# Mamba stage of a decoder kernel: silu taken by ScalarE's own function, the residual added by TensorE, the x product and GpSimd's share of the read-outs moved

## The reference, cut to what matters

```python
residual = hidden + residual
hidden = _layernorm(residual, norm_w[i], norm_b[i])
xin, z = jnp.split(jnp.einsum('bld,ed->ble', hidden, in_w), 2, axis=-1)   # 2 x 256 channels
xc = silu(causal_conv(xin, cw, cb))                                       # 4 taps
dtr, Bm, Cm = split(jnp.einsum('bld,ed->ble', xc, xp_w))                  # 8, 16, 16
dt = softplus(jnp.einsum('blr,dr->bld', dtr, dtp_w) + dtp_b)
h = exp(dt * A) * h + (dt * xc) * B        # a scan over time, for 16 states
y = sum over the 16 states of h * C, + xc * D
hidden = jnp.einsum('bld,ed->ble', y * silu(z), out_w)
```

## Time and profile before

| | |
|---|---|
| time, three runs | 8373.63 / 8380.08 / 8388.14 us |
| time of the profiled execution | 8408.26 us |
| its span, first to last instruction | 8406.3 us |
| mean granted clock of PE | 0.856 of full speed |
| busy in the whole span | PE 76%, DVE 80%, ACT 52%, POOL 58% |
| Mamba rounds | from 112.0 to 4187 us, 64 rounds |

### The profile page before, as it was taken

How to read it: one execution, slowest core, us unless ns; L and a number is a source line. 1 busy time by engine, 2 the same in 40 slices (tenths; PEclk the granted TensorE clock), 3 DMA queues, 4 the chain that set the end, 5 groups by cost and what they waited for, 6 DMA issues and landing times. The chain is left out here.

```text
span 8406.3 us, 94285 instructions
## 1 busy us (share of the span) xinstructions
PE 6429.7 (76%) x25844; PEld 3390.0 (40%) x25859; DVE 6708.0 (80%) x15635; ACT 4403.6 (52%) x9194; POOL 4877.1 (58%) x2829
## 2 busy tenths in 40 slices
PE   5888888888888888888789967777656777777745
PEld 2333333333333333333355545555433444455522
DVE  5999999999999999999855558888666767767657
ACT  3555555555555555555555523333325666666633
POOL 4888878888788888888744434444212333333310
PEclk9998899889888889988889978888757989989955
DMA  5333333333433333333310047777310000000011
GB/s 183 136 149 157 138 145 143 152 143 145 156 135 149 153 141 139 146 157 135 143 32 26 20 122 204 206 205 204 109 44 17 10 9 9 9 9 9 6 32 36
DMA packets 373729, 896.56 MB, mean 107 GB/s; under 512 B 28031, under 2 KB 270076, under 8 KB 306972
## 3 DMA queue, kind: packets, MB, share of 16 engines
q1 hardware_dynamic: 332508, 692.64, 22.0%
q0 software_dynamic: 40960, 201.36, 8.3%
HBM read 850.58 MB, written 56.77 MB: 108 GB/s over the span
## 5 line engine op out<-in xcount | busy, mean ns | idle before, releaser
L380 POOL TENSOR_TENSOR mb_dBu<-mb_dtu,mb_rows_b 128x1024 f32<-128x1024 f32 x1027 | 2406.5, 2361 | 360.9 <-DVE mb_bank L394 186.5
L394 DVE TENSOR_TENSOR_SCAN mb_bank<-mb_bank,mb_dBu 128x1024 f32<-128x1024 f32 x704 | 1612.7, 2291 | 71.8 <-PEq L63 50.9
L434 PE MATMUL mb_bank<-mb_hcd,ident 128*128 128x512 f32 x2560 | 1269.6, 623 | 76.7 <-DVE mb_hcd L408 76.7
L365 ACT ACTIVATE mb_bank<-mb_dt,mb_a_neg 128x508 f32<-128x508 f32 x2050 | 1312.4, 671 | 0.8
L434 PE MATMUL mb_bank<-mb_hcp,ident 128*128 128x512 f32 x1280 | 792.5, 752 | 366.2 <-POOL mb_hcp L417 366.2
L417 POOL TENSOR_TENSOR mb_hcp<-mb_hs,mb_rows_c 128x1024 f32<-128x1024 f32 x320 | 753.0, 2353 | 354.9 <-DVE mb_hs L394 351.7
L408 DVE TENSOR_TENSOR mb_hcd<-mb_bank,mb_rows_c 128x1024 f32<-128x1024 f32 x704 | 862.1, 1225 | 31.3
L434 PEld LDWEIGHTS mb_bank<-mb_hcd,ident 128*128 128x128 f32 x2560 | 501.3, 202 | 793.3 <-issue 588.4
L1542 POOL DMA_INDIRECT ex_rows<-in_ex_table,ex_idx x512 | 490.1, 957 | 560.3 <-DVE ex_idx L1538 345.2
L394 DVE TENSOR_TENSOR_SCAN mb_hs<-mb_bank,mb_dBu 128x1024 f32<-128x1024 f32 x320 | 730.9, 2284 | 40.1 <-ACT mb_bank L365 40.1
L434 PEld LDWEIGHTS mb_bank<-mb_hcp,ident 128*128 128x128 f32 x1280 | 282.0, 234 | 815.2 <-POOL mb_hcp L417 494.7
(11 more groups left out here) (369 smaller groups left out, 13434.8 us busy)
## 6 DMA issues: line engine op xcount, KB each, us to landing
mb_rows_b<-bc_rows SPq DMA_DIRECT2D x259, 1024.0 KB, 7.4
mb_rows_c<-bc_rows SPq DMA_DIRECT2D x258, 1024.0 KB, 6.8
stream<-mb_r_post SPq DMA_DIRECT2D x69, 256.0 KB, 2.4
mb_r_tok<-stream SPq DMA_DIRECT2D x67, 256.0 KB, 2.8
mb_r_post<-stream SPq DMA_DIRECT2D x65, 256.0 KB, 2.8
ex_rows<-in_ex_table,ex_idx POOLq DMA_INDIRECT x512
tj_x_tok<-stream SPq DMA_DIRECT2D x17, 256.0 KB, 3.1
bc_rows<-mb_xp SPq DMA_DIRECT2D x65, 64.0 KB, 1.6
```

The lines of the kernel that those rows point to most:

```text
L365: e = nc.scalar.activation(da_of(n)[:, c * GB:(c + 1) * GB, 1:], dt[q][:, c].rearrange("p (b t) -> p b t", b=GB)[:, :, 1:], ACT.Exp, scale ...
L380: nc.gpsimd.tensor_tensor(by_c(dBu[m % RING][:]), by_c(chains(dtu[q][:])), over_c(rows_b[:, n]), ALU.mult).then_inc(s["mb_dbu"], 1)
L394: nc.vector.tensor_tensor_scan(flat(to), flat(da_of(n)), flat(dBu[n % RING][:]), 0.0, ALU.mult, ALU.add).then_inc(s["mb_scan"], 1)
L434: m = nc.tensor.matmul(bank[:, B_Y + c], ident[:], part[:, c * GB:(c + 1) * GB], start=False, stop=False)
```

## The change

In the Mamba stage alone:

- Silu of the convolution is one ACT instruction per half with function Silu, straight into `u`; both stand after step 3's `act_da`. `dve_conv` is gone. Silu of z is one ACT instruction over both halves; `dve_z` is gone. The weights lose their factors.
- The residual is added by PE: a product of the identity with the old rows (`r_old`, a buffer of its own) opens the accumulation in bank `M1`, ahead of `pe_out`. ACT copies the sum out (`act_new`, after its step 1) in place of DVE's addition.
- PE's convolution of the second half stands right after `pe_out`, ahead of the skip products, and the x product after the sum of step 2 (it was after step 4's place).
- POOL reads out the states 1, 5, 8, 10 and 12 (they were 2, 4, 8, 10 and 12).

```diff
-ON_POOL = (2, 4, 8, 10, 12)
+ON_POOL = (1, 5, 8, 10, 12)
...
             def act_conv(self, act, c):
                 act.wait_ge(s["mb_conv"], c + 1)
-                nc.scalar.activation(th[:, c], bank[:, M0 + c], ACT.Tanh, scale=0.5, bias=conv_bh[:, c:c + 1]).then_inc(s["mb_tanh"], 1)
-                act.wait_ge(s["mb_tanh"], c + 1)
-                nc.scalar.activation(th[:, c], th[:, c], ACT.Identity, bias=1.0).then_inc(s["mb_th"], 1)
...
+                nc.scalar.activation(u[self.q][:, c], bank[:, M0 + c], ACT.Silu, bias=conv_b[:, c:c + 1]).then_inc(s["mb_u"], 1)
...
             def act_z(self, act):
...
+                act.wait_ge(s["mb_z"], CH)
+                nc.scalar.activation(zg[self.q][:], x_psum, ACT.Silu).then_inc(s["mb_zg"], 1)
...
             def pe_out(self, pe):
+                pe.wait_ge(s["mb_rp"], 16)
+                nc.tensor.matmul(bank[:, M1], ident[:], r_old[:].rearrange("p b d -> p (b d)"), start=True, stop=False)
                 pe.wait_ge(s["mb_yg"], 1)
...
-            def dve_add(self, dve):
-                dve.wait_ge(s["mb_out"], 1)
-                dve.wait_ge(s["mb_rp"], 16)
...
+            def act_new(self, act):
+                act.wait_ge(s["mb_out"], 1)
+                nc.scalar.activation(r_post[:].rearrange("p b d -> p (b d)"), bank[:, M1], ACT.Copy).then_inc(s["mb_new"], 1)
...
                         if n == 1:
-                            ahead.act_conv(act, 0)
+                            behind.act_new(act)
                         if n == 3:
-                            ahead.act_conv(act, 1)
+                            for c in range(CH):
+                                ahead.act_conv(act, c)
...
                     behind.pe_out(pe)
+                    pe.wait_ge(s["mb_new"], 1)
+                    ahead.pe_conv(pe, 1)
                     scan.pe_skip(pe)
...
-                        if n == 1:
-                            pe.wait_ge(s["mb_new"], 1)
-                            ahead.pe_conv(pe, 1)
...
-                        if n == 4:
+                        if n == 2:
                             ahead.pe_x(pe)
```

More of the change, by code:

```diff
@@ L91, in mamba_stage @@
         out_raw, w_out = (sb(n, [P, CH, D]) for n in ("out_raw", "w_out"))
-        conv_bh, conv_b = sb("conv_bh", [P, CH]), sb("conv_b", [P, CH])
+        conv_b = sb("conv_b", [P, CH])
         norm_wb = sb("norm_wb", [P, 2])
@@ L105, in mamba_stage @@
         h_ch = sb("h_ch", [P, GB, KW])
-        th, zth = sb("th", [P, CH, TOK]), sb("zth", [P, CH, TOK])
         xp = sb("xp", [2 * DS + DR + 1, TOK])
         ab, ey, ln1, small = (sb(n, [P, CH, TOK]) for n in ("ab", "ey", "ln1", "small"))
-        dt, dtu, u2, zg = (pair(n, [P, CH, TOK]) for n in ("dt", "dtu", "u2", "zg"))
+        dt, dtu, u, zg = (pair(n, [P, CH, TOK]) for n in ("dt", "dtu", "u", "zg"))
         rows_b, rows_c = sb("rows_b", [P, DS, TOK]), sb("rows_c", [P, DS, TOK])
@@ L144, in _ @@
                 nc.vector.memset(xp[2 * DS:2 * DS + DR + 1, :], 1.0)
-                nc.vector.memset(u2[1][:], 0.0)
+                nc.vector.memset(u[1][:], 0.0)
                 nc.vector.memset(zg[1][:], 0.0)
@@ L224, in pe_x @@
                 for c in range(CH):
-                    m = nc.tensor.matmul(bank[0:2 * DS + DR, M0], w_x[:, c], u2[self.q][:, c], start=(c == 0), stop=(c == CH - 1))
+                    m = nc.tensor.matmul(bank[0:2 * DS + DR, M0], w_x[:, c], u[self.q][:, c], start=(c == 0), stop=(c == CH - 1))
                 m.then_inc(s["mb_xp"], 1)
@@ L286, in act_z @@
             def act_z(self, act):
-                for c in range(CH):
-                    act.wait_ge(s["mb_z"], c + 1)
-                    nc.scalar.activation(zth[:, c], bank[:, M0 + c], ACT.Tanh, scale=0.5).then_inc(s["mb_zth"], 1)
-            def dve_z(self, dve):
-                for c in range(CH):
-                    dve.wait_ge(s["mb_zth"], c + 1)
-                    nc.vector.scalar_tensor_tensor(out=zg[self.q][:, c], in0=zth[:, c], scalar=1.0, in1=bank[:, M0 + c],
-                                                   op0=ALU.add, op1=ALU.mult).then_inc(s["mb_zg"], 1)
+                act.wait_ge(s["mb_z"], CH)
+                nc.scalar.activation(zg[self.q][:], x_psum, ACT.Silu).then_inc(s["mb_zg"], 1)
         class Behind:
@@ L421, in pe_skip @@
                 for c in range(CH):
-                    nc.tensor.matmul(bank[:, B_Y + c], skip[:, c], u2[self.q][:, c], start=True, stop=False)
+                    nc.tensor.matmul(bank[:, B_Y + c], skip[:, c], u[self.q][:, c], start=True, stop=False)
             def pe_sum(self, pe, n):
@@ L517, in _ @@
                 dve_skip(dve)
-                for c in range(CH):
-                    first.dve_conv(dve, c)
                 first.dve_poly(dve)
@@ L522, in _ @@
                 first.dve_dt(dve)
-                first.dve_z(dve)
                 dve.wait_ge(s["mb_res"], 2 * 16)
@@ L643, in _ @@
                             behind.dve_gate(dve)
-                        if n == 1:
-                            behind.dve_add(dve)
-                        if n == 2:
-                            ahead.dve_conv(dve, 0)
-                        if n == 4:
-                            ahead.dve_conv(dve, 1)
                         if n == 6 and shape == 0:
-                            nc.vector.tensor_scalar(w_out[:], out_raw[:], 0.25, None, ALU.mult).then_inc(s["mb_wo"], 1)
+                            nc.vector.tensor_copy(w_out[:], out_raw[:]).then_inc(s["mb_wo"], 1)
                         if n == 6 and shape == GROUPS - 2:
@@ L664, in _ @@
                             ahead.dve_dt(dve)
-                        if n == 12:
-                            ahead.dve_z(dve)
                 @block.tensor
@@ L715, in _ @@
                 last.dve_gate(dve)
-                last.dve_add(dve)
+            @block.scalar
+            def _(act):
+                last.act_new(act)
             @block.tensor
```

21 lines of the change are left out of this document (6 added, 15 removed).

## The result

The changed kernel takes 8326.21 us (median of five runs, 8321.87 to 8329.84), the kernel before took 8373.63 beside it (five runs, 8363.17 to 8388.14). The ratio is 0.9947, with an interval of 0.9935 to 0.9958: half a per cent faster. The forecast was 8345 with a range of 8270 to 8420 and "faster" at 0.58. The time came within 20 us of the forecast, though its terms for the middle and the tail of a round were off by 32 and 17 us and the term for its end was missing.

What follows compares the result with a forecast made beforehand. PE's chain, then ACT, was taken to set the start of a round, not DVE. Terms of -21, -44 and +28 gave -37 us: 8408.3 to 8371, less 28 for the median, 8343, rounded 8345; range 8270 to 8420.

Steps and rivals of the forecast that it cites:

- the middle: From step 8's scan to dt: PE's shorter hole keeps its clock up in four rounds in ten, -44 us.
- the tail: From dt to step 13's scan: the table load back to the exponentials behind z's silu costs +28 us.
- the term for its end: From step 13's scan to the next round: the prediction's sum had no term for this stretch.
- Which engine bounds: In the Mamba rounds: DVE isn't the bound everywhere; PE, then ACT, sets steps 8 and 10.
- the first rival: In all Mamba rounds: DVE is the bound after all, 198 us saved, 8182 us; chance 0.07.
- Head: From a round's start to step 8's scan: 0 in most rounds, as PE's row keeps its length; -21 us by eleven rounds.
- eleven rounds: Rounds with convolution weights, skip matrices or output weights' copy, where DVE is late at step 8: -1.9 us each, -21 us.
- 53 plain ones: The rounds outside the eleven rounds; their stretch up to step 8's scan was costed at 0.
- the slower rival: z's table load delays step 13, and a 0.85 us hole makes more rounds begin at low clock: 8457 at most; chance 0.21.
- the rival in which the clock stays up: PE's clock ahead of dt stays up in nearly all rounds, POOL would be next: 8277 us; chance 0.15.

Runs made afterwards that it cites:

- e8: The changed kernel with one product of the identity with zeros on PE behind step 14's sum, ahead of the barrier: 8343.9 us, ratio 0.9928 to the kernel before.
- e6: The changed kernel with three products of the identity with zeros in PE's hole ahead of step 8's sum: 8275.85 us, ratio 0.9865 to the kernel before.
- e3: The changed kernel with Tanh in place of Silu for z, so without the two table loads there: 8272.3 us, ratio 0.9845 to the kernel before.
- e9: The changed kernel with three products with zeros ahead of step 8's sum and one behind step 14's: 8242.73 us, ratio 0.9858 to the kernel before.
- e10: e9 with PE's transposes of the next block ahead of the sums of steps 12 and 13: 8251.63 us, ratio 0.9861 to the kernel before.
- e12: The changed kernel with three products with zeros ahead of step 8's sum and Tanh for Silu on z: 8264.58 us, ratio 0.9859 to the kernel before.

## Why the prediction was right, and where its terms were wrong

**Which engine bounds: right.** Taking 145 us from DVE gave 62 in the rounds, not the 198 of the first rival.

**Head: right in size, by luck in part.** Predicted were 0 in most rounds and -21 us by eleven rounds; the table gives 0.37 x 64 = -24. Of these -14 are in the eleven rounds (their mean head falls from 33.18 to 31.90) and -10 in the 53 plain ones, where the cause was not forecast: fewer of them begin at the low clock (15 instead of 24). PE's row came out as worked out: 24.7 us to the first dt product against 24.6, with a hole of 0.69 for the copy, and the plain rounds' median is 30.19 us against 30.05. But step 8's scan waits 1.28, not 2.1. Of the missing 0.8 us, 0.66 are the epsilon addition (0.83 instead of 0.17 in the round shown), which is held up because POOL's new order has it at work there, and 0.18 are a new wait of step 7's scan for ACT. The prediction looked at who waits for POOL's read-outs and not at what runs on DVE beside them. The changed kernel's low starts are not caused by its 0.69 us hole, as the slower rival had it, since e8 takes nearly all away by filling the hole ahead of the barrier and leaves that one.

**Middle: right in mechanism, too small.** The hole is 2.95, predicted 2.8. The prediction took four rounds in ten with the clock up, -44 us. The table gives 1.19 x 64 = -76; the wait at dt fell by 144.7 - 68.5 = 76.2 us, where 120 are all that can fall (144.7 - 25.2, e6). So it was more than six in ten of the whole. e6 shows that the stall at dt is the clock after this hole. e8 shows that with a hole of 2.95 us it goes either way from one execution to the next (101.9 us at dt), so the size of this term is a draw and could not be worked out from the rows. One reading of the rows was too simple: after the 4.55 us hole the sum is whole at the low clock (3.78 us) in 48 of 64 rounds of the kernel before, and in the other 16 it takes 2.98 us or more, so there the clock comes back within it; in none does it take 1.98.

**Tail: right in mechanism, too large.** Predicted +28, measured 0.17 x 64 = +11. The load behind z's zeros is there, without a pause behind it. The scan of 13 comes 7.53 to 8.82 us after dt, where the prediction had 7.50 with a fast z and 8.84 with a slow one; in the round shown it is 1286.02 - 1278.48 = 7.54. The counts are what failed: z ended late (5 us after dt) in 12 rounds instead of 37, but early (3.3 us) in only 2 instead of 18, and in between in 50. The prediction had used the counts of the kernel before.

**End: missing.** The prediction's sum stops at step 13's scan. It takes it, without a word, that what stands behind this scan moves with it, and so puts the end of a round at nothing. The measured +0.42 x 64 = +27 us are DVE's longer wait at the barrier (77 us instead of 50.9). Step 12's sum waits for POOL, whose work from the read-out of step 10 to that of step 12 takes 9.2 us however early dt is, and PE's transposes and ACT's last work wait for that sum. The prediction named POOL as next only in the rival in which the clock stays up, with its 2.82 us of idle time before a round, and did not follow what PE and ACT do behind its last read-out. This +27 happened to cancel most of the middle's extra gain of 32 us. With the head's 3 and the tail's 17 us better than forecast, the rounds came to -62 in the table for a sum of -37, and the medians to -47.

That gains in between are lost at the barrier is measured: from step 8's scan to the next round pass 32.41 us before, 31.81 in the changed kernel, and 31.28 to 31.51 in e3, e6, e9, e10 and e12, though their waits and loads in between differ by more than 1 us. That POOL's chain is what sets this floor is read from the traces alone (11.62 to 11.70 us from step 10's scan to the read-out of step 12 in the changed kernel and in these five); no run shortened it.

**The version to keep** is e6 or e9: 0.9865 and 0.9858, not told apart. Moving one of POOL's instructions between steps 10 and 12 to another engine was not tried.

## What to carry to other kernels

Work out, for each stretch of a round, which chain comes second and by how much, up to the barrier and not only up to the next scan: here 27 us came back at the barrier, from a term that the sum did not have. When GpSimd's order is changed, look at which small instructions of VectorE run beside it at the new time. And where TensorE idled for some 3 us ahead of work on the path, three products with zeros in the hole were worth about as much again as the whole change (by the ratios 0.8% against 0.5, by the table's rounds 38 us against 62), and a product taken off TensorE there gained nothing.

## What the runs showed of the hardware

- A DVE instruction on 4 columns from SBUF to SBUF, 0.17 us alone, took 0.81 to 0.91 us when a GpSimd tensor_tensor was running (52 of 64 rounds of the changed kernel), and ended 0.028 us behind it (median). The Trainium skill (SBUF — State Buffer, "SBUF: two separate sides") says that DVE and GpSimd share a port pair as an exclusive lock: the one that starts first holds it for its whole instruction while the other blocks, if the DVE instruction has two SBUF inputs or runs in a mode that uses two ports. The trace agrees with the blocking; this instruction has one SBUF input, and whether it ran in such a mode no run here shows. DVE's scans, which read PSUM and SBUF, were not stretched (2.29 us in either kernel).
- The granted clock after a hole on PE, told by the time of step 8's sum (1.98 us at 2.4 GHz, 3.78 at 1.2). After 4.28 to 4.67 us it took 2.98 to 3.78 in every round of the kernel before; after 2.95 it took 1.98 in 38 of 53 rounds of the changed kernel and in 9 of 55 of e8, and up to 3.78 in the others; after 0.37 to 1.72 it took 1.98 in every round (e6). With both holes filled the low stretch stood in another place (e9: z's product 3.78 us).
- A table load took 1.28 us and the next function started 0.01 us behind it, also between silu and exponentials; and the load does not wait with its function (it starts at 1279.58 us and its function, which waits for PE, at 1282.30), but it does wait behind the zeros ahead of it (1283.22 and 1283.40).
